# Graph layer with a mixture-of-experts feed-forward on one core: dense sets of four tiles begin every seven tiles instead of every eight

## The reference, cut to what matters

```
def gnn(x, W, bias, edge_row, edge_col, edge_val):
    h = x @ W
    msgs = h[edge_col] * edge_val[:, None]
    return segment_sum(msgs, edge_row, num_segments=12500) + bias

def ffn(x, gamma, beta, Wr, br, W1, b1, W2, b2):        # x is 12500 x 256
    xn = (x - mean(x)) * rsqrt(var(x) + 1e-5) * gamma + beta
    top_vals, top_idx = top_k(xn @ Wr + br, 2)
    w_full = softmax(top_vals) spread over the 8 experts
    y = 0
    for e in range(8):
        y += (gelu(xn @ W1[e] + b1[e]) @ W2[e] + b2[e]) * w_full[:, e]
    return y

x = x + gnn(layernorm(x), W, bias, src, dst, edge_weight)
return x + ffn(layernorm(x), ...)
```

## Time and profile before

| | us |
|---|---|
| median of 3 runs | 3982.83 |
| the profiled execution's own time | 3981.84 |
| its span (first to last instruction) | 3979.7 |
| span until PE closes tile 0 (L1837) | 936.7 |
| until PE closes tile 97 | 3344.9 |
| until PE begins the first block | 3474.3 |
| until the last block's rows are copied | 3917.6 |

### The profile page before, as it was taken

One profiled execution on the slowest core, in us unless ns is written; L12 is line 12 of the kernel. 1 busy time (PEld: TensorE's weight loads), 2 busy tenths in 40 slices (PEclk: granted clock), 3 DMA queues, 4 the chain that ended last, 5 costly groups with the idle time before them and its releaser, 6 DMA issues.

```text
span 3979.7 us, 75949 instructions
## 1 busy us (share of the span) xinstructions
PE 3194.3 (80%) x20888; PEld 2076.7 (52%) x20888; DVE 2415.8 (61%) x6037; ACT 1331.0 (33%) x2857; POOL 2538.3 (64%) x2491
## 2 busy tenths in 40 slices
PE   6677767824788899898988998998988989099983
PEld 4444444412455555555555555555555556088862
DVE  9699334514666666666666666676666665144563
ACT  1354656720222222222222222222222222066651
POOL 1241457877777777777777777777777776630264
PEclk9899989966899999999999999999999999599996
DMA  4341110003434334434343434343334346552463
GB/s 154 106 117 60 33 36 15 8 12 92 117 110 119 110 113 114 119 112 120 112 117 110 117 110 120 109 115 108 114 111 120 108 118 104 175 165 86 125 202 113
DMA packets 288427, 420.20 MB, mean 106 GB/s; under 512 B 89733, under 2 KB 218314, under 8 KB 288138
## 3 DMA queue, kind: packets, MB, share of 16 engines
q0 software_dynamic: 109280, 279.33, 25.2%
q1 hardware_dynamic: 112536, 72.81, 6.4%
q10 hardware_dynamic: 66324, 64.42, 5.1%
HBM read 339.36 MB, written 76.98 MB: 105 GB/s over the span
## 4 chain that ended last, share of the span: by engine, by line
PE 36%; DVE 14%; issue 11%; POOL 7%; DVEq 5%; DMA 2%; ACT 1%; SPq 1%; ACTq 0%; POOLq 0%
PE twin L1902 7%; PE twin L1832 6%; PE bank L1902 6%; POOL area L798 5%; DVE area L1395 3%; PE twin L1834 3%; DVEq L1410 2%; DVE area L1403 2%; PE twin L1885 2%; PE bank L1885 2%; PE twin L1970 2%; PE twin L1987 2%; POOL zs L815 2%; PE bank L1970 1%; PE bank L1987 1%
## 5 line engine op out<-in xcount | busy, mean ns | idle before, releaser
L798 POOL DMA_INDIRECT area<-h_table,listed x1856 | 1864.3, 1004 | 606.0 <-issue 542.9
L1832 PE MATMUL twin<-area 128*128 x2608 | 880.9, 385 | 76.7 <-POOLq L797 38.3
L1834 PE MATMUL twin<-area 128*128 x2608 | 718.2, 275 | 0.0
L973 ACT ACTIVATE area<-twin,b_t 128x512 f32<-128x512 f32 x192 | 132.0, 687 | 1446.0 <-PE twin L1885 860.2
L1403 DVE TENSOR_TENSOR area<-area,listed 128x1024 f16 x652 | 422.6, 689 | 106.9 <-DVE area L1395 94.9
L1832 PEld LDWEIGHTS twin<-area 128*128 x2608 | 257.0, 99 | 415.2 <-issue 183.3
L766 POOL DMA_INDIRECT edge_list<-area,didx x256 | 313.0, 1223 | 77.1 <-issue 77.1
L1902 PE MATMUL twin<-w2h,area 128*128 128x256 f16 x1536 | 338.6, 317 | 0.0
L751 POOL TENSOR_TENSOR area<-area 128x256 f16<-128x256 f32 x98 | 80.9, 829 | 339.8 <-ACT area L862 339.6
L1834 PEld LDWEIGHTS twin<-area 128*128 x2608 | 257.1, 99 | 49.1 <-issue 0.2
L1902 PE MATMUL bank<-w2h,area 128*128 128x256 f16 x1536 | 267.7, 273 | 0.0
(11 more groups left out here) (339 smaller groups left out, 6505.3 us busy)
## 6 DMA issues: line engine op xcount, KB each, us to landing
area<-h_table,listed POOLq DMA_INDIRECT x1856
area<-in_x_dram SPq DMA_DIRECT2D x194, 128.0 KB, 2.2
area<-zs SPq DMA_DIRECT2D x66, 256.0 KB, 2.9
ys<-area ACTq DMA_DIRECT2D x66, 256.0 KB
out_dram<-area ACTq DMA_DIRECT2D x100, 128.0 KB, 2.6
h_table<-area SPq DMA_DIRECT2D x97, 128.0 KB, 1.7
xt<-in_x_dram ACTq DMA_DIRECT2D x97, 128.0 KB
area<-in_L_ffn_W_dram ACTq DMA_DIRECT2D x16, 512.0 KB, 4.0
```

Source lines behind the costliest of these rows:

```text
L798: pool.indirect_dma_start(out=stage[:, (k % RU) * UNIT + 2 * D * c:(k % RU) * UNIT + 2 * D * (c + 1)], out_offset=None, in_=h_table[:, :], ...
L973: nc.scalar.activation(h32[:, m, :], psH[m][:, :], ACT.Gelu, scale=1.0 / WSCALE, bias=b1_t[:, e * KH + m:e * KH + m + 1])
L1832: nc.tensor.matmul(psA[:, :], target[:, ds(at, P, 2)], stage[:, ds(rows, 2 * D)], start=False, stop=False)
L1834: last = nc.tensor.matmul(psA[:, 0:D], target[:, ds(at + TGT // 2, P, 2)], stage[:, ds(rows, D)], start=False, stop=False)
```

## The change

Sets begin at tiles 0, 7, 14, ..., 84 and at tile 94: 14 sets of four, 56 dense tiles, 112 jobs, 42 routed tiles. A set's first two jobs now belong to the same step, four behind its first tile, and the other six to the six steps after it; those of the last set take steps 98 to 105, one each. The first job of a step keeps its place; the second comes at the end of the step on each engine, behind the logits, `top2` and `choose`. R0 becomes 28, the parts 28 and 14 tiles, the blocks 36 + 22 = 58. Steps 95, 96 and 97 have a tile and no job. `LAST` becomes the tiles of places 27 and 41, the latter tile 93.

```diff
@@ -100,10 +101,18 @@
...
     SB = 4
-    NSET = NT // (2 * SB)
+    CYCLE = 7
+    begins = list(range(0, NT - CYCLE, CYCLE)) + [NT - SB]
+    NSET = len(begins)
+    set_of = {b + q: (c, q) for c, b in enumerate(begins) for q in range(SB)}
     NEX = NSET * NE
+    jobs = {}
+    for i in range(NEX):
+        c, e = divmod(i, NE)
+        jobs.setdefault(begins[c] + SB + (e * CYCLE // NE if c + 1 < NSET else e), []).append(i)
+    STEPS = max(jobs) + 1
     NHC = NE * KH
-    routed = [t for t in range(NT) if t % (2 * SB) >= SB or t >= 2 * SB * NSET]
+    routed = [t for t in range(NT) if t not in set_of]
     place_of = {t: j for j, t in enumerate(routed)}
@@ -950,8 +959,8 @@
...
                 reached(act, s_lgm, t - 1)
-                q, c = t % (2 * SB), t // (2 * SB)
-                dense = t not in place_of
+                dense = t in set_of
+                c, q = set_of.get(t, (0, 0))
                 if dense:
@@ -992,7 +1001,7 @@
...
                 else:
-                    r, q = c * 2 * SB * P - PAD, 0
+                    r, q = begins[c] * P - PAD, 0
                 act.dma_start(out[r:r + (SB - q) * P, :].rearrange("(q p) d -> p q d", p=P),
@@ -1005,22 +1014,26 @@
...
             act.dma_start(xt[0][PAD:P, :], x[0:P - PAD, :]).then_inc(s_xl[0], 16)
-            for t in range(NT + SB - 1):
-                i = t - SB
+            def apply_expert(i):
+                if i > NE and i % NE == 1:
+                    store_set(i // NE - 1)
+                if i % NE == 0:
+                    weights_T(i // NE)
+                gelus(i)
+
+            for t in range(STEPS):
                 if t + 1 < NT:
...
                     store_routed(t - 1)
-                if i > NE and i % NE == 1:
-                    store_set(i // NE - 1)
-                if 0 <= i < NEX:
-                    if i % NE == 0:
-                        weights_T(i // NE)
-                    gelus(i)
+                for i in jobs.get(t, [])[:1]:
+                    apply_expert(i)
                 if t < NT:
                     transposed(t)
-                    if t % (2 * SB) == SB - 1 and t // (2 * SB) < NSET:
-                        exps(t // (2 * SB))
+                    if t in set_of and set_of[t][1] == SB - 1:
+                        exps(set_of[t][0])
+                for i in jobs.get(t, [])[1:]:
+                    apply_expert(i)
             store_set(NSET - 1)
@@ -1464,14 +1477,14 @@
...
             def x_low(t):
-                q, c = t % (2 * SB), t // (2 * SB)
+                c, q = set_of[t]
                 dve.wait_ge(s_xTh, t + 1)
...
             def top2(t):
-                dense = t not in place_of
-                q = t % (2 * SB)
+                dense = t in set_of
+                c, q = set_of.get(t, (0, 0))
                 biggest, which = (mx[:, q, :], ix[:, q, :]) if dense else (mxr[:, :], ixr[:, :])
@@ -1598,8 +1611,14 @@
...
 
+            def sum_expert(i):
+                h_low(i)
+                if i >= 1:
+                    add_expert(i - 1)
+                if i % NE == 0:
+                    add_b2(i // NE)
+
             def step(t):
-                i = t - SB
                 if t < NT:
@@ -1613,21 +1632,19 @@
...
                         back_rows(LAST.index(t - 1))
-                if 0 <= i < NEX:
-                    h_low(i)
-                if 1 <= i <= NEX:
-                    add_expert(i - 1)
-                if 0 <= i < NEX and i % NE == 0:
-                    add_b2(i // NE)
+                for i in jobs.get(t, [])[:1]:
+                    sum_expert(i)
                 if t < NT:
...
                         choose(t)
-                    elif t % (2 * SB) == SB - 1:
-                        differences(t // (2 * SB))
-                        finalise(t // (2 * SB))
+                    elif set_of[t][1] == SB - 1:
+                        differences(set_of[t][0])
+                        finalise(set_of[t][0])
+                for i in jobs.get(t, [])[1:]:
+                    sum_expert(i)
 
@@ -1642,8 +1659,9 @@
...
             ahead(0)
-            for t in range(NT + SB + 1):
+            for t in range(STEPS):
                 step(t)
+            add_expert(NEX - 1)
 
@@ -1838,9 +1856,9 @@
...
             def transposes(t):
-                c = (t - SB) // (2 * SB)
-                if c >= 0:
-                    pe.wait_ge(s_wT, min(c + 1, NSET))
+                before = len([b for b in begins if b + SB <= t])
+                if before:
+                    pe.wait_ge(s_wT, before)
                 reached(pe, s_lgc, t)
@@ -1904,7 +1922,7 @@
...
             def weights_T(c):
-                t = c * 2 * SB + SB
+                t = begins[c] + SB
                 pe.wait_ge(s_wf, c + 1)
@@ -1924,24 +1942,32 @@
...
             pe.wait_ge(s_clear, 1)
-            for t in range(NT + SB + 1):
-                i = t - SB
+            def sum_before(i):
+                if i >= 1:
+                    expert(i - 1)
+                if i % NE == 0:
+                    b2_terms(i // NE)
+
+            for t in range(STEPS):
+                now = jobs.get(t, [])
                 if t < NT:
...
                     ranks(t - 1)
-                if 0 <= i < NEX and i % NE == 0:
-                    weights_T(i // NE)
-                if 0 <= i < NEX:
+                for i in now[:1]:
+                    if i % NE == 0:
+                        weights_T(i // NE)
                     hidden(i)
...
                     transposes(t)
-                if 1 <= i <= NEX:
-                    expert(i - 1)
-                if 0 <= i < NEX and i % NE == 0:
-                    b2_terms(i // NE)
+                for i in now[:1]:
+                    sum_before(i)
                 if t < NT:
                     logits(t)
+                for i in now[1:]:
+                    hidden(i)
+                    sum_before(i)
+            expert(NEX - 1)
 
...
             w2h_e, w2l_e = (w[:, :, :, :].rearrange("p e k n -> p (e k n)") for w in (w2h, w2l))
```

## The result

| us | before | after |
|---|---|---|
| median (four runs each, on one chip) | 3983.57 | 4014.57 |
| lowest to highest | 3973.16 to 3984.86 | 4007.92 to 4016.71 |
| the profiled execution's span | 3979.7 | 4012.9 |

The ratio of after to before is 1.0081, 95% interval 1.006 to 1.0101: the change makes the kernel 0.8% slower.

What follows compares the result with a forecast made beforehand. The prediction took a PE-DVE chain to pace the node stage, with POOL close behind. Node stage +121.5, gap -6, blocks and end -62.7 gave +53 us, a forecast of 4035 us, range 3990 to 4070.

Steps and rivals of the forecast that it cites:

- What bounds the kernel: Node stage: a chain between PE and DVE paces each step, with POOL following close behind.
- Rival 1: Node stage: POOL paces it and the extra jobs are free, giving 3914 us; chance 0.06.
- The second job at 10.5 us: End of a two-job step: the job overlaps nothing and costs PE's full time; 13 such jobs, +136.5 us.
- -10 for step 4: Step 4's second job fills step 5's 9.0 us wait for first gathers, with 1 us more behind: -10 us.
- Rival 2: Node stage: the second job lies largely beside DVE's chain, 3.4 us each, giving 3956 us; chance 0.10.
- rival 3: Node stage: DVE's 4.6 us of each second job adds to PE's time, giving 4095 us; chance 0.08.
- DVE leaves such a step earlier, -6: Two-job steps: DVE leaves about 0.8 us earlier against PE, shrinking two thirds of 12 `zb` waits: -6 us.
- The other terms of the node stage, +1: Node stage: extra set's start +4, steps 95 and 96 without job -7, block table in step 94 +4 us.
- The gap, -6: Tile 97 to first block: 123 us instead of 129.4, job chain a few us later than scatters: -6 us.
- The blocks and the end, -62.7: After the gap: eight fewer blocks -49.4, five fewer part 0 tiles -3.7, three fewer part 1 tiles -9.6 us.
- The clock: Node stage: longer unbroken PE work might keep the clock up, saving 22 us for 4013; not taken.
- The sum: Whole kernel: node stage 121.5, gap -6, blocks and end -62.7, together +53 us.

Runs made afterwards that it cites:

- Six steps without a job: Kernel before with its twelfth set begun at tile 94, one job a step, none in steps 92 to 97: 3975.84 us, ratio 0.9991 to before.
- the tighter cycle: The change without the set at tile 94, thirteen sets every seven tiles: 4048.03 us, ratio 1.0174 to the kernel before.
- the early layer: The change with the second job's first layer moved ahead of the transposes on PE: 3975.85 us, ratio 0.9997 to the kernel before.
- the late sums: The change with DVE's low parts and sums of a second job moved behind the next step's targets: 3997.57 us, ratio 1.0038 to before.

## Why the prediction was right, by its own steps

**What bounds the kernel: right.** PE and DVE pace the node stage together and POOL follows. Thirteen more jobs on PE, one of them covered in step 4, moved the stage by 113.7 us with the gathers as they were, and what POOL gained was slack: the expected 100 us more of waiting for a free unit were 104. Rival 1 (POOL paces) is refuted by the same number. The rule of the Trainium skill beside it (Perfetto Trace Analysis, Identifying the Most-Contended Engine) picks the engine with the highest occupancy, by the prediction's reading POOL. This case does not bear it out: PE was busy for 90% of the stage and POOL had 98% of it taken with its issue gaps, and the waits, not the shares, told which one was behind.

**The second job at 10.5 us: right.** Measured 10.5 in its own step. The forecast's +136.5 with -10 for step 4 is +126.5 for twelve; the runs show 125.7. The cover in step 4 was there too: the period from tile 4 to 5 is 32.2 us with two jobs (1027.62 to 1059.78) and the wait for POOL of the earlier trace rows is gone; without the second job tile 5 closes no earlier (1061.9). Rival 2 (3.4 us each) and rival 3 (4.6 more) are both out. Rival 2 had more in it than the forecast gave: not at the place that the change chose, but with the first layer ahead of the transposes the kernel keeps 3 us of each job.

**DVE leaves such a step earlier, -6: too small.** The steps behind gave back 11.4 us, 8.5 of it as less wait for `zb`: eight of the twelve steps waited, as the two thirds of the step have it, but each by 1.1 us less and not 0.8. The shorter second layers behind such waits (2.2 us) had no term.

**The other terms of the node stage, +1: too high.** Without the second jobs tile 97 closes 6.7 us before that of the earlier trace rows (3338.2 against 3344.9), for a forecast of 4 - 7 + 4 = +1. At tile 94, up to where only the extra set's start counts (+4), it was already 3.2 us ahead (3266.6 against 3269.8); from there to tile 97 it gained 3.5, as the -7 and +4 have it. The term that was off is thus the +4 for the set's start: one more set's b2 terms, transposes and `finalise` cost nothing that shows. Which of these small items lay under a wait was not tried one by one.

**The gap, -6: right.** 122.7 us for a forecast of 123, with PE busy for 95 of them, and the last set's cover is shown by the run without it: the first block came within 0.1 us of the same time, though behind 60 scatters. The job chain was right nearly step by step: fills at 107.3 us and 15.7 more were forecast, 107.1 and 15.6 measured. The scatters were put at 1.29 us each, where the earlier trace rows give 85.3 / 65 = 1.31 and the change has 1.34. The forecast had the job chain a few us later than the scatters; SP's wait of 1.1 us for DVE's clearing shows it the later one by that much. Uncovered, the set would have cost some 95 us, the step said; it was never run uncovered, but PE's 85 us more of work beside the scatters are that cover.

**The blocks and the end, -62.7: a little too small.** Measured -67.1. The end was -9.5 (14 tiles in 45 us) for -9.6. From the first block to the last copied row it went from 443.3 to 385.8, -57.5 for a forecast of -53.1. One early block period, with PE waiting for its load of `zs`, was 10.35 us before (3.12 of it that wait) and 7.63 after (1.67), which is 2.7 of the 4.4 us; 1.7 are unexplained.

**The clock: right, and 4013 is chance.** The prediction's other course, a clock that stays up over the next wait, would have given 4013, and 4014.57 was measured; still, that is not what happened. Right behind the two-job steps, in steps 12, 47 and 89, waits of 2.94, 2.46 and 2.92 us were each followed by transposes and a second layer of 7.1 to 7.3 us, at a granted clock of 0.77 to 0.79; where the wait was under 1 us they took 5.65 us, at 1.00. Without second jobs the same three steps took 7.0 to 8.5 us, behind waits of 3.8 to 4.5. Over the whole stage 36 steps took more than 6.3 us for this in the change and 34 without second jobs, and the mean granted clock is 0.96 before and after. So the longer unbroken work did not keep the clock up over the next wait. The length of the wait does not decide it alone: before the change, step 68 waited 2.91 us and took 5.65 at a clock of 1.00. The Trainium skill (TensorE: Matmul & The Clock Gate, Part 1) says that activity releases the throttle and idleness brings it back; the second half agrees with step 46, 6.80 us behind 2.78 us of idle PE and 5.13 with none.

**The sum.** By the spans the change is +33.2 us where the sum said +53, and the difference is in the small terms: 5.4 in what DVE gave back, 7.7 in the other terms, 4.4 in the blocks and the end, 0.7 in the gap, and some 1.5 in the second jobs with the start and end of the stage. All of them erred to the same side, and the range was wide enough for it.

## What to carry to other kernels

Work that is added to a stage paced by two engines in turn costs its full time where it stands back to back with the rest, and less where it is put ahead of the instruction that waits: look for each engine's longest wait, and put there what doesn't depend on what the wait is for. A stretch in which an engine idles for transfers can take a whole batch of its work for nothing, and that is worth having apart from the rest of a change: here the last set gained 33 us while the tighter cycle lost 66. The gains of two moves need not add, even where each shortens a wait of its own: the early layer took away the PE time beside which the late sums had gained, and the second move is to be judged in the order that the first one leaves.

## What the runs showed that I had not expected

Six steps without a job ended the node stage only 11.1 us sooner: with PE relieved, its waits for gathers came up (13.2 us in six pieces, up to 7.5 us). POOL is a close second limit. The price of an idle wait on PE is higher than the wait: in the two-job steps 26.1 us of waits taken away brought 37.0 us. And a control stretch on DVE stands ahead of nearly each tile's targets, 2.3 to 3.5 us long in the change and 225.3 us in 75 pieces over its node stage; no kernel here changed it, so what it is worth is not shown, and it is what is left to try.
